# U turned onto the feature partitions by TensorE, and the first loads regrouped, in a two-layer conditioned residual kernel

## The chip, the cores and the metric

One NeuronCore of a Trainium2 chip. The metric is the device time of one execution in microseconds. The kernel before took 618.98 us (median of 3 runs, 617.96 to 619.11).

## The reference

B = 2, S = 2048, D = 512, RANK = 30. Two layers, each added to its input:

```python
# layer 0: a linear map of low rank that depends on the batch
U = (cond_512 @ W_dec + b_dec).reshape(B, 513, 30)     # cond_512 [2, 256], W_dec [256, 15390]
param = einsum('bik,kj->bij', U, V)                    # V [30, 512]
x = x + einsum('bsd,bde->bse', x, param[:, :-1]) + param[:, -1][:, None]
# layer 1: six views of x, concatenated, through an MLP with layer norms
h = ln(ln(x, pw_g[path], pw_b[path]), cp_g[comp], cp_b[comp])
t = ln(x, tm_g[comp], tm_b[comp]);  s = ln(x, ms_g[scale], ms_b[scale])
m, n, r = (x + mlp_ln(state)[:, None] for state in (cond_512, cond_64, fside))
w = softmax(aw)
x = x + mlp_ln(concat([w[0]*h, w[1]*t, w[2]*m, w[3]*n, w[4]*r, w[5]*s]))   # W1 [3072, 512], W2 [512, 512]
```

## The kernel before

The 4096 rows are 32 tiles of 128 rows, alternating between the batches. Five engines each run an instruction list written out by hand and meet only at semaphores; the order in each list is the order of the work. Products that need accuracy are three float32r products (high x high, high x low, low x high) of 128x512; small set-up products are plain f32.

Start-up on TensorE, in its order (L759 to L955):
- 16 decode steps (`decode`, L724). Each multiplies cond, 32 columns per chunk, with a 960 KB block of W_dec (four concurrent products of 480 columns). Two steps make one eighth of U as rows: partition c*32+b holds batch b of feature chunk c. ScalarE copies each eighth to `Ur` (`evacuate`, L546).
- Behind nine of the steps a `prefill` (L749): twelve products of the x part of layer 1 for tiles 2 to 13. The x weights are the sum of the m, n and r blocks of W1, scaled by the softmax (`wx_first` L521 on ScalarE, `wx_add` L1166 and `wx_low` L1174 on VectorE), from the 12 tiles `mnr`.
- Then prefill 9, the first MLP product (L774, L775), prefill 10, the transposes of its result (L877), `embed` of tile 0 (L794), which needs the stacked U (`Ust`), prefill 11, `expand` of tile 0 (L804), the second MLP products (L866) and the phases of tiles 0 to 2. `sum_parts` (L873), `low_rank_product` (L885) and `offset_product` (L897) stand between them.

U has to stand with features on the partitions. `to_features` (L376) does that with 16 transfers, each from one row of `Ur` to 64 partitions with 30 numbers each: eight when half of U has been copied, eight when all has. GpSimd issues 12 of them before its other work, ScalarE 4. VectorE then adds the bias (L1234) and writes the stack (L1237, L1239) that `embed` needs.

For tile 0, VectorE sums x1 (L1276) and takes its statistics (L1249, L1253); GpSimd makes 1/sqrt from the variance (L1021 to L1034), but only after the low halves of x of tiles 0 and 1 (`x_low`, L1070); ScalarE makes xhat (L640); VectorE scales it to tt and st; TensorE transposes these (L737).

Loads: SP's queue carries the 12 mnr tiles, then W_dec blocks mixed with x^T tiles (`stash`), the MLP weights, the T, S and H blocks of W1 and W2 as ring slots come free, and for each tile x, its indices and index rows (`idxrep`, two broadcasts to 64 partitions). ScalarE's queue carries aw, all constants (`cst`, 1203 columns: cond, identity, bias, V^T, then the picking matrices and others), V, wlast and the MLP biases.

Of the kernel before, what the change touches and what calls it, by code (L numbers as in the profile page):

```python
# [25 lines left out]
ALU = mybir.AluOpType  # L26
# [5 lines left out]
RANK = 30  # L32
# [95 lines left out]
def build(nc, d, out):  # L128
# [11 lines left out]
    with ExitStack() as ctx:  # L140
# [46 lines left out]
        aw = sb("aw", [P, 6])  # L187
# [62 lines left out]
        mnr = sb_at(at_mnr, "mnr", [P, 3, KC, D])  # L250


        V4, wlast = stash[:, NPRE - 1, :], stash[:, NPRE - 2, 0:2 * P].rearrange("p (c r) -> p c r", r=P)
# [18 lines left out]
        XU, XV = bank[0:2]  # L272
        TP, HID, OUT = bank[2:4], bank[4:6], bank[6:8]
# [6 lines left out]
        aw_in, cst_in, late_in, mlp_in = sem("aw_in"), sem("cst_in"), sem("late_in"), sem("mlp_rows_in")  # L280
# [8 lines left out]
        u_in_pool, u_in_act = sem("u_in_pool"), sem("u_in_act")  # L289
# [86 lines left out]
        def to_features(eng, got, half, rows):  # L376

            eng.wait_ge(u_row, DECS // 2 * (half + 1))
            at, n = half * P // 2, P // 2
            load(eng, got, *[(Uf[at:at + n, b, c, :],  # L380
                              Ur[c * Q + b:c * Q + b + 1, at * RANK:(at + n) * RANK].rearrange(
                                  "o (p r) -> o p r", r=RANK)) for c, b in rows])

        U_ROWS = [(c, b) for c in range(KC) for b in range(B)]

# [4 lines left out]
        def _(sp):  # L390
# [26 lines left out]
            def load_rows(a):  # L417
# [15 lines left out]
                for half in range(2):  # L433
                    sp.dma_start(idxrep[half * P // 2:(half + 1) * P // 2, s, :],
                                 d["rows"][s, half, bass.ds(pair, 1), :].to_broadcast([P // 2, P])) \
                      .then_inc(rep_in[s], 16)

            for c in range(KC):
                for k, src in enumerate((WM, WN, WR)):
                    load(sp, mnr_in[c], (mnr[:, k, c, :], d["int_W1"][src * D + c * P:src * D + (c + 1) * P, :]))  # L440
            for j in range(2 * DECS):
# [18 lines left out]
            load_x(Tile(1))  # L460
            sp.wait_ge(dec_used, 2 * DECS)
# [48 lines left out]
        def _(act):  # L510
            load(act, aw_in, (aw[:, :], d["aw"].to_broadcast([P, 6])))
            load(act, cst_in, (cst[:, :], d["cst"]))
            load(act, late_in, (V4, d["V4"]), (wlast, d["wlast"].rearrange("(c p) r -> p c r", p=P)))
# [7 lines left out]
            def wx_first(c):  # L521
                act.wait_ge(mnr_in[c], 48)
                nc.scalar.activation(wx[:, c, :], mnr[:, 0, c, :], ACT.Copy, scale=wsm[:, WM:WM + 1]).then_inc(wx_m, 1)
# [52 lines left out]
            to_features(act, u_in_act, 1, U_ROWS[KC:])  # L576
# [146 lines left out]
        def _(pe):  # L723
# [34 lines left out]

            pe.wait_ge(cst_in, 16)  # L759
            for j in range(2 * DECS):  # L760
                decode(j)
                if j == 0:

                    pe.wait_ge(late_in, 32)
# [105 lines left out]
            def sum_parts(sel, got, done, start=True):  # L870

                pe.wait_ge(got, 1)
# [7 lines left out]
            def low_rank_product():  # L880

                pe.wait_ge(lm_ready, 2)
                for k in range(3):
                    for c in range(KC):
                        nc.tensor.matmul(pPART[c * Q:(c + 1) * Q, :], LM[:, k, c, :], mnr[:, k, c, :],  # L885
# [5 lines left out]
            def offset_product():  # L891

                pe.wait_ge(vw_part, 1)
# [113 lines left out]
        def _(pool):  # L1007
# [85 lines left out]
            to_features(pool, u_in_pool, 0, U_ROWS)  # L1093
# [508 lines left out]
```

## Time and profile before

| | |
|---|---|
| profiled execution | 619.02 us, its span 617.2 us |
| TensorE busy | 586.1 us, 95% |
| GpSimd, VectorE, ScalarE busy | 390.1, 417.5, 204.2 us |
| mean granted clock of TensorE | 0.997 |
| HBM over the span | 164 GB/s |
| first product of TensorE | 18.06 us |

PE is TensorE, PEld its weight loads, DVE VectorE, ACT ScalarE, POOL GpSimd, SP the engine that issues most transfers; SPq, ACTq and POOLq are the issues of a transfer. L731 is line 731 of the kernel before. A group of instructions names the tile written and the tiles read. A plain f32 product appears as two weight loads and two multiplies. Times count from the start of the span. `ring` holds W_dec and later weights, `bank` is PSUM.

### The profile page before, as it was taken

The numbers are of one execution on the slowest core, as the hardware profiler recorded it, in microseconds if no ns is written. First come the engines' busy times: TensorE is split into PE (matmuls) and PEld (weight loads), VectorE is DVE, ScalarE is ACT, GpSimd is POOL, SyncE is SP. The second block draws the span as 40 slices with busy tenths as digits, with TensorE's granted clock in tenths as the row PEclk, the third lists the DMA queues.
The fourth block names the chain that finished last, engine by engine and source line by source line (L and its number), as shares of the span: only waits on it lengthen the run. The fifth ranks groups of instructions, "written<-read, shape, count | busy, mean of one in ns | idle before, by whom it ended". The sixth has DMA issues, their size and how long they took to land.

```text
span 617.2 us, 9159 instructions
## 1 busy us (share of the span) xinstructions
PE 586.1 (95%) x2924; PEld 454.5 (74%) x2924; DVE 417.5 (68%) x750; ACT 204.2 (33%) x346; POOL 390.1 (63%) x499
## 2 busy tenths in 40 slices
PE   0899979999999999999999999999999999999995
PEld 0455436488888888888888888788888888888784
DVE  3411277588888888888766766776666666667754
ACT  3333344334333334333232233233223332332222
POOL 1002447668888888888776667666776766666720
PEclk9999999999999999999999999999999999999998
DMA  8999898434454455555424344445443433344201
GB/s 292 404 403 381 302 356 282 126 90 140 142 172 145 142 148 159 172 157 176 146 90 122 121 139 140 109 139 140 140 130 99 135 125 123 124 140 112 81 19 51
DMA packets 53119, 102.07 MB, mean 165 GB/s; under 512 B 10446, under 2 KB 23246, under 8 KB 52956
## 3 DMA queue, kind: packets, MB, share of 16 engines
q1 hardware_dynamic: 39872, 58.52, 28.0%
q0 software_dynamic: 12160, 42.04, 22.3%
q10 hardware_dynamic: 1052, 1.07, 0.5%
q8 instruction: 18, 0.29, 0.2%
q14 instruction: 17, 0.14, 0.1%
HBM read 93.10 MB, written 8.39 MB: 164 GB/s over the span
## 4 chain that ended last, share of the span: by engine, by line
PE 68%; POOL 7%; issue 7%; DMA 7%; DVE 6%; SPq 2%; ACT 2%; POOLq 0%; DVEq 0%; ACTq 0%
PE bank L743 18%; PE bank L744 18%; PE bank L745 18%; PE bank L737 7%; DMA xraw<-in_xT 2%; PE bank L731 2%; DMA ring<-in_W_dec 2%; DMA ring<-in_int_W 2%; PE bank L794 2%; SPq L332 2%; DVE bn L1249 2%; POOL rs L1029 1%; POOL h L1081 1%; POOL h L1079 1%; POOL ctt L1046 1%
## 5 line engine op out<-in xcount | busy, mean ns | idle before, releaser
L743 PE MATMUL bank<-W,ops 128*128 128x512 f32 x432 | 178.4, 413 | 0.1
L744 PE MATMUL bank<-W,ops 128*128 128x512 f32 x432 | 171.4, 397 | 0.0
L745 PE MATMUL bank<-W,ops 128*128 128x512 f32 x432 | 171.1, 396 | 0.0
L591 ACT ACTIVATE ops<-bank 128x512 fp32r<-128x512 f32 x97 | 57.0, 589 | 154.1 <-PE bank L737 152.4
L743 PEld LDWEIGHTS bank<-W,ops 128*128 128x128 f32 x432 | 81.8, 189 | 25.4 <-issue 7.3
L745 PEld LDWEIGHTS bank<-W,ops 128*128 128x128 f32 x432 | 81.7, 189 | 20.0
L744 PEld LDWEIGHTS bank<-W,ops 128*128 128x128 f32 x432 | 81.9, 190 | 14.8
L1244 DVE TENSOR_TENSOR ops<-bank,ops 128x512 fp32r<-128x512 f32 x97 | 66.1, 683 | 11.7 <-ACT ops L591 11.7
L1249 DVE BATCH_NORM_STATS2 bn<-h 128x6 f32<-128x512 f32 x32 | 22.2, 692 | 55.2 <-POOL h L1081 55.2
L1021 POOL TENSOR_SCALAR ve<-mv 128x1 f32<-128x1 f32 x94 | 31.4, 334 | 38.5 <-DVE mv L1253 34.8
L640 ACT ACTIVATE xhat<-x,nm,rs 128x512 f32<-128x512 f32 x32 | 26.1, 815 | 81.0 <-POOL nm L1034 81.0
L743 PE MATMUL bank<-W,zop 128*128 128x512 f32 x124 | 49.6, 400 | 0.4 <-DVE zop L1244 0.4
L1081 POOL TENSOR_TENSOR h<-h,pwt 128x512 f32<-128x512 f32 x32 | 47.6, 1488 | 2.5
L744 PE MATMUL bank<-W,zop 128*128 128x512 f32 x124 | 49.0, 395 | 0.0
L745 PE MATMUL bank<-W,zop 128*128 128x512 f32 x124 | 49.0, 395 | 0.0
L1070 POOL TENSOR_TENSOR xop<-stash,xop 128x512 fp32r<-128x512 f32 x18 | 23.2, 1289 | 39.5 <-ACT xop L562 39.5
L1370 DVE SCALAR_TENSOR_TENSOR o<-o,mv,gbc 128x512 f32<-128x512 f32 x31 | 47.6, 1537 | 0.0
L1046 POOL DMA_INDIRECT ctt<-in_ct,idx x32 | 40.6, 1270 | 9.4 <-issue 5.9
L1079 POOL TENSOR_TENSOR h<-xhat,pwt 128x512 f32<-128x512 f32 x32 | 42.7, 1335 | 2.9 <-ACT xhat L640 1.9
L647 ACT ACTIVATE ht<-h,nm,rs 128x512 f32<-128x512 f32 x32 | 26.1, 816 | 55.2 <-POOL nm L1034 55.2
L332 POOL DMA_DIRECT2D Uf<-Ur x12 | 6.5, 563 | 58.6 <-ACT Ur L548 58.6
L1046 POOL DMA_INDIRECT sgt<-in_ms_g,idx x32 | 35.4, 1105 | 11.4 <-issue 11.4
(145 smaller groups left out, 1089.3 us busy)
## 6 DMA issues: line engine op xcount, KB each, us to landing
ring<-in_W_dec SPq DMA_DIRECT2D x16, 960.0 KB, 12.5
x<-in_x SPq DMA_DIRECT2D x32, 256.0 KB
out<-xb SPq DMA_DIRECT2D x31, 256.0 KB
stash<-in_xT SPq DMA_DIRECT2D x30, 256.0 KB, 6.3
ring<-in_int_W SPq DMA_DIRECT2D x4, 1024.0 KB, 11.7
xraw<-in_xT SPq DMA_DIRECT2D x14, 256.0 KB
mnr<-in_int_W SPq DMA_DIRECT2D x12, 256.0 KB, 8.0
idxrep<-in_rows SPq DMA_DIRECT2D x64, 32.0 KB
```

The costliest lines, as they stand in the source:

```text
L591: nc.scalar.activation(dst.rearrange("p c t -> p (c t)"), bank[:, :], ACT.Copy).then_inc(done, 1)
L737: last = nc.tensor.transpose(dst[:, c * P:(c + 1) * P], src[:, c * P:(c + 1) * P], ident)
L743: nc.tensor.matmul(bank[:, :], op[:, HI, c, :], w[:, HI, c, :], start=start and c == 0, stop=False)
L744: nc.tensor.matmul(bank[:, :], op[:, HI, c, :], w[:, LO, c, :], start=False, stop=False)
L745: last = nc.tensor.matmul(bank[:, :], op[:, LO, c, :], w[:, HI, c, :], start=False, stop=stop and c == KC - 1)
L1021: nc.gpsimd.tensor_scalar(ve[:, which:which + 1], mv[:, which, 1:2], EPS, 1.0, ALU.add, ALU.mult) \
L1046: pool.indirect_dma_start(out=dst[:, s, :], out_offset=None, in_=d[table], in_offset=bass.IndirectOffsetOnAxis(ap=idx[:, s, col:col + 1], ...
L1079: nc.gpsimd.tensor_tensor(h1[:, :], xhat[:, :], pwt[:, s, 0:D], ALU.mult).then_inc(h1_part, 1)
L1081: nc.gpsimd.tensor_tensor(h1[:, :], h1[:, :], pwt[:, s, D:2 * D], ALU.add).then_inc(h1_ready, 1)
L1244: nc.vector.tensor_tensor(dst.rearrange("p c t -> p (c t)"), bank[:, :], hi.bitcast(F32).rearrange("p c t -> p (c t)"), ALU.subtract).then ...
L1249: nc.vector.bn_stats(bn[:, which, :], src).then_inc(bn_done, 1)
L1370: nc.vector.scalar_tensor_tensor(out=o[:, :], in0=o[:, :], scalar=mv[:, 2, 0:1], in1=gbc[:, :], op0=ALU.subtract, op1=ALU.mult).then_inc(u ...
```

## The change

The sixteen transfers go. After the last decode step TensorE waits until all of U has been copied and multiplies: for each of the 30 ranks r, the weights are the 128 columns `Ur[:, p*30 + r]` (a step of 30 numbers), the moving operand eight columns of the identity, which pick the rows c*32+b. The results stand in one PSUM bank; VectorE reads them there when it adds the bias. The low halves of stash tiles 10 and 11 (`pre_low`), made ahead of the stack of U until now, are made behind it.

mnr is stored in the order of loading: 4 loads of 768 KB with 6 KB rows, not 12 of 256 KB. aw stands ahead of the first (64 bytes per row, 16 numbers), already repeated on 128 rows. The constants are loaded in two parts by SP: columns 0 to 507 ahead of the last mnr load, the rest (`picks_in`) after tile 1's x; four places wait for it. V and wlast become one load behind the first W_dec block. The index rows are stored repeated, one load of 128 rows per tile. Stash tiles 10 and 11 are loaded ahead of tile 0's rows.

```diff
+        URT = bank[0][:, 0:RANK * B * KC]
-        def to_features(eng, got, half, rows):
-            eng.wait_ge(u_row, DECS // 2 * (half + 1))
...
+            def turn_u():
+                pe.wait_ge(u_row, DECS)
+                for r in range(RANK):
+                    last = nc.tensor.matmul(URT[:, r * B * KC:(r + 1) * B * KC],
+                                            Ur.rearrange("q (p r) -> q r p", r=RANK)[:, r, :],
+                                            ident.rearrange("p (c q) -> p q c", q=Q)[:, 0:B, :], start=True, stop=True)
+                last.then_inc(u_turned, 1)
...
                 if j in PRE_AFTER:
                     prefill(PRE_AFTER.index(j))
+            turn_u()
             prefill(NPRE - 3)
...
# SP
-            for c in range(KC):
-                for k, src in enumerate((WM, WN, WR)):
-                    load(sp, mnr_in[c], (mnr[:, k, c, :], d["int_W1"][...]))
+            load(sp, mnr_in[0], (mnr_row[:, 0:P // 8 + 3 * D], d["mnr"][:, 0:P // 8 + 3 * D]))
+            for c in range(1, KC):
+                if c == KC - 1:
+                    load(sp, cst_in, (cst[:, 0:AT_BL], d["cst"][:, 0:AT_BL]))
+                load(sp, mnr_in[c], (mnr[:, c, :, :], d["mnr"][...]))
...
                 load_ring(sp, DEC[j])
+                if j == 0:
+                    load(sp, late_in, (late, d["late"]))
...
-            load_rows(Tile(0))
             load_pre(NPRE - 2)
             load_pre(NPRE - 1)
+            load_rows(Tile(0))
...
             load_x(Tile(1))
+            load(sp, picks_in, (cst[:, AT_BL:CST], d["cst"][:, AT_BL:CST]))
# ScalarE
-            load(act, aw_in, (aw[:, :], d["aw"].to_broadcast([P, 6])))
-            load(act, cst_in, (cst[:, :], d["cst"]))
-            load(act, late_in, (V4, d["V4"]), (wlast, d["wlast"]...))
-            to_features(act, u_in_act, 1, U_ROWS[KC:])
# GpSimd
-            to_features(pool, u_in_pool, 0, U_ROWS)
-            to_features(pool, u_in_pool, 1, U_ROWS[:KC])
# VectorE
-            v.wait_ge(aw_in, 16)
+            v.wait_ge(mnr_in[0], 16)
-            for p in range(2, NPRE - 1):
+            for p in range(2, NPRE - 2):
                 pre_low(p)
-            pre_low(NPRE - 1)
-            v.wait_ge(u_in_pool, 16 * 3 * KC)
-            v.wait_ge(u_in_act, 16 * KC)
+            v.wait_ge(u_turned, 1)
             for b in range(B):
-                last = nc.vector.tensor_tensor(Uf[:, b, :, :], Uf[:, b, :, :], bdec[:, :, :], ALU.add)
+                last = nc.vector.tensor_tensor(
+                    Uf[:, b, :, :], URT.rearrange("p (r b c) -> p b c r", b=B, c=KC)[:, b, :, :], bdec[:, :, :], ALU.add)
...
+            pre_low(NPRE - 2)
+            pre_low(NPRE - 1)
```

## Rows read from the trace of the kernel before

**Rows 1.** The page's first part: busy us, share of the span, instructions.

```profile
PE 586.1 (95%) x2924; PEld 454.5 (74%) x2924; DVE 417.5 (68%) x750; ACT 204.2 (33%) x346; POOL 390.1 (63%) x499
```

**Rows 2.** TensorE's waits, 0 to 140 us: us in total, times, longest.

```profile
PE bank L731 <- DMA ring<-in_W_dec: 18.7, 3, 18.1
PE bank L873 <- ACT part L595: 2.4, 2, 1.5
PE bank L794 <- POOL xop L1070: 1.5, 1, 1.5
PE bank L866 <- DMA ring<-in_mem_W: 0.8, 1, 0.8
PE bank L794 <- DVE Ust L1239: 0.6, 1, 0.6
```

**Rows 3.** Busy time by stretch; last: granted clock, DMA share, GB/s.

```profile
2.00:5.00 3.00, 0.00 (x0) 0.00 (x0) 0.00 (x0) 0.90 (x1) 0.51 (x3) 1.00 0.65 148
8.00:16.00 8.00, 0.00 (x0) 0.00 (x0) 5.11 (x8) 3.67 (x6) 0.00 (x0) 1.00 1.06 384
16.00:50.00 34.00, 31.72 (x157) 17.46 (x158) 10.51 (x19) 11.52 (x22) 3.49 (x7) 1.00 1.05 403
50.00:55.00 5.00, 5.00 (x26) 3.17 (x26) 0.69 (x1) 1.59 (x3) 0.92 (x2) 1.00 1.07 367
66.00:69.00 3.00, 3.00 (x11) 1.31 (x11) 0.00 (x0) 0.00 (x0) 2.18 (x5) 1.00 0.52 135
```

**Rows 4.** Timeline of TensorE's decode steps: start us, us, what, wait before.

```profile
21.06 1.83 PE L731 MATMUL bank<-ring,cst 128*32 128x480 f32 x8 [0.22 <-DMA ring<-in_W_dec]
63.62 1.01 PE L731 MATMUL bank<-ring,cst 128*32 128x480 f32 x8 [0.37 <-DMA ring<-in_W_dec]
```

**Rows 5.** Transfer issues, 0 to 140 us: count, KB each, median us to landing.

```profile
ring<-in_W_dec SPq DMA_DIRECT2D x16, 960.0 KB, 12.5
mnr<-in_int_W SPq DMA_DIRECT2D x12, 256.0 KB, 8.0
...
cst<-in_cst ACTq DMA_DIRECT2D x1, 601.5 KB, 6.5
...
stash<-in_V ACTq DMA_DIRECT2D x1, 256.0 KB, 7.4
```

**Rows 6.** Timeline of VectorE: the last two low halves of wx.

```profile
17.88 1.47 DVE L1176 TENSOR_TENSOR W<-wx,W 128x512 fp32r<-128x512 f32 x2
```

**Rows 7.** Timeline of ScalarE: the last copy of U's sums.

```profile
64.70 0.57 ACT L548 ACTIVATE Ur<-bank 128x480 f32<-128x480 f32 x1 [1.10 <-PE bank L731]
```

**Rows 8.** Timelines of TensorE and its weight loads (PEld): f32 loads, grouped.

```profile
19.82 1.01 PE L766 MATMUL bank<-cst,stash 128*128 128x2 f32 x4
...
75.13 0.32 PEld L877 LDWEIGHTS bank<-cst,part 6*128 6x128 f32 x4 [0.37 <-issue]
...
111.16 0.30 PEld L873 LDWEIGHTS bank<-part,cst 128*128 128x128 f32 x2
```

**Rows 9.** Groups of weight loads, 0 to 140 us: busy us, mean ns of one.

```profile
L873 PEld LDWEIGHTS bank<-part,cst 128*128 128x128 f32 x4 | 0.6, 188 | 1.1 <-issue 1.1
...
L877 PEld LDWEIGHTS bank<-cst,part 6*128 6x128 f32 x4 | 0.3, 136 | 0.4 <-issue 0.4
```

**Rows 10.** Timelines of VectorE and GpSimd: tile 0's sums, variance, tile 1's low half.

```profile
80.42 0.68 DVE L1276 TENSOR_TENSOR x<-bank,x 128x512 f32<-128x512 f32 x1
81.94 0.18 DVE L1253 BATCH_NORM_AGGREGATE mv<-bn 128x2 f32<-128x6 f32 x1
...
81.97 1.26 POOL L1070 TENSOR_TENSOR xop<-xraw,xop 128x512 fp32r<-128x512 f32 x1 [8.52 <-ACT xop L562]
```

**Rows 11.** Chain that ended last: start us, us, what.

```profile
24.04 0.43 PE bank L745
...
29.68 0.24 PE bank L744
```

**Rows 12.** Busy time by stretch at the kernel's end, columns as in rows 3.

```profile
613.00:614.00 1.00, 0.00 (x0) 0.00 (x0) 0.92 (x2) 0.29 (x1) 0.00 (x0) 0.87 0.53 199
```

More of the change, by code:

```diff
@@ L249, in build @@
         assert cursor[0] - at_mnr >= 3 * BLOCK
-        mnr = sb_at(at_mnr, "mnr", [P, 3, KC, D])
-        V4, wlast = stash[:, NPRE - 1, :], stash[:, NPRE - 2, 0:2 * P].rearrange("p (c r) -> p c r", r=P)
+        mnr_row = sb_at(at_mnr - 4 * P // 8, "mnr_row", [P, P // 8 + KC * 3 * D])
+        aw, mnr = mnr_row[:, P // 8 - 6:P // 8], mnr_row[:, P // 8:].rearrange("p (c k n) -> p c k n", k=3, n=D)
+        late = stash[:, NPRE - 2:NPRE, :].rearrange("p a n -> p (a n)")[:, D - 2 * P:2 * D]
+        V4, wlast = late[:, 2 * P:2 * P + D], late[:, 0:2 * P].rearrange("p (c r) -> p c r", r=P)
         def x_rows(a):
@@ L374, in u_bank_of @@
             return pU[m % len(pU)]
-        def to_features(eng, got, half, rows):
-            eng.wait_ge(u_row, DECS // 2 * (half + 1))
[L379 to L384, printed above, removed]
         block = ctx.enter_context(nc.Block())
@@ L432, in load_rows @@
                     sp.wait_ge(oh_ready, read)
[L433 to L436, printed above, removed]
-            for c in range(KC):
-                for k, src in enumerate((WM, WN, WR)):
-                    load(sp, mnr_in[c], (mnr[:, k, c, :], d["int_W1"][src * D + c * P:src * D + (c + 1) * P, :]))
+                sp.dma_start(idxrep[:, s, :], d["rows"][s, bass.ds(pair, 1), :, :].rearrange("o p n -> (o p) n")) \
+                  .then_inc(rep_in[s], 16)
+            load(sp, mnr_in[0], (mnr_row[:, 0:P // 8 + 3 * D], d["mnr"][:, 0:P // 8 + 3 * D]))
+            for c in range(1, KC):
+                if c == KC - 1:
+                    load(sp, cst_in, (cst[:, 0:AT_BL], d["cst"][:, 0:AT_BL]))
+                load(sp, mnr_in[c], (mnr[:, c, :, :], d["mnr"][:, P // 8 + c * 3 * D:P // 8 + (c + 1) * 3 * D].rearrange(
+                    "p (k n) -> p k n", n=D)))
             for j in range(2 * DECS):
@@ L521, in wx_first @@
             def wx_first(c):
-                act.wait_ge(mnr_in[c], 48)
-                nc.scalar.activation(wx[:, c, :], mnr[:, 0, c, :], ACT.Copy, scale=wsm[:, WM:WM + 1]).then_inc(wx_m, 1)
+                act.wait_ge(mnr_in[c], 16)
+                nc.scalar.activation(wx[:, c, :], mnr[:, c, 0, :], ACT.Copy, scale=wsm[:, WM:WM + 1]).then_inc(wx_m, 1)
             def wx_high(c):
@@ L1344, in split_bt @@
             def split_bt():
+                v.wait_ge(picks_in, 16)
                 v.wait_ge(bt_high, 1)
@@ L1577 @@
         "idx": np.stack([path, comp, scale], axis=-1),
-        "rows": np.stack([scale, comp], axis=1),
+        "rows": np.repeat(np.stack([scale, comp], axis=2), P // 2, axis=2),
         "cst": cst,
         "int_b1": L1["int_b1"][None], "int_b2": L1["int_b2"][None], "int_g": L1["int_g"][None],
-        "int_be": L1["int_be"][None], "aw": L1["aw"][None],
+        "int_be": L1["int_be"][None],
+        "mnr": np.concatenate([np.zeros((P, P // 8 - 6), np.float32), np.broadcast_to(L1["aw"][None], (P, 6)), np.stack(
+            [chunks(L1["int_W1"][src * D:(src + 1) * D]) for src in (WM, WN, WR)], axis=2).reshape(P, -1)], axis=1),
         "mlp_W1": chunks(put(2 * MU, D, (0, 0, L1["mem_W1"]), (MU, 0, L1["noi_W1"]), (MU + P, 0, L1["res_W1"]))),
@@ L1584 @@
         "mlp_b2": np.repeat(np.stack([L1[f"{m}_b2"] for m in mlps]), B, axis=0),
-        "wlast": put(MU, P, *[(0, q * Q, W_dec[:, NDEC:]) for q in (0, 2, 3)]),
         "W_dec": W_dec,
-        "V4": put(P, D, *[(q * Q, 0, V) for q in range(4)]),
+        "late": np.concatenate([flat(chunks(put(MU, P, *[(0, q * Q, W_dec[:, NDEC:]) for q in (0, 2, 3)]))),
+                                put(P, D, *[(q * Q, 0, V) for q in range(4)])], axis=1),
         "pw": np.concatenate([L1["pw_g"], L1["pw_b"]], axis=1),
```

23 lines of the change are left out of this document (12 added, 11 removed).

## The prediction

> **What bounds the kernel now.** I read the page's busy shares first, then TensorE's waits in the first 140 us, then the chain, the transfer rates by stretch, and the timelines of each engine from 61 to 110 us.
>
> TensorE is busy for 95% of the span [rows 1]. Its waits over 0.5 us are few and all lie early: 18.7 us for W_dec (18.1 of them before its first product), 2.4 for the copied partial sums, 1.5 for the low half of tile 1's x, 0.8 for the second MLP's weights and 0.6 for the stacked U [rows 2]. From 125 us on it hardly waits, so the steady part moves as a block: what TensorE loses or wins before 110 us is the whole change in time. I therefore look for how much later or earlier it reaches tile 1's transposes (about 110 us), where the start-up ends.
>
> The start is bound by transfers. They move 148 GB/s from 2 to 5 us, 384 from 8 to 16 and 403 later [rows 3]; TensorE's second decode step waits until 21.06 us for its block of W_dec and the first prefill follows at once [rows 4]. From there to 61 us it never waits for over 0.1 us. The transfers keep pace, and only the last block is late: 0.37 us at 63.62 [rows 4].
>
> **Part 1, the order of the first loads.** Ahead of the second W_dec block the queues carry 12 x 256 KB of mnr, 601.5 of constants, 256 of V, about 31 small, and 960 + 960 of W_dec [rows 5], with 128 of wlast (256 x 128 numbers) and 256 of x (128 x 512): 6264 KB. After the change the constants are cut at column 508 of 1203, 254 KB, and the rest (347 KB) goes behind tile 1's x; aw adds 8 KB of padding and rides in the first wide load; V and wlast are one load of 384 behind the first block. That is 5922 KB. 342 KB less at 403 GB/s [rows 3] brings the second decode step 0.87 us forward. The first decode step gains more (726 KB, 1.8 us), but the prefill stands behind the second. The softmax of aw now waits for the 776 KB of the first wide load, at latest about 6 us; the chain of wx on ScalarE and VectorE then runs on, and has to end before the 20.2 at which the block lands. It was over at 19.35 before [rows 6], with nearly 1 MB more mixed into its loads, so even without the gain it is hidden.
>
> **Part 2, wide first loads.** Twelve issues become four, and the 128-row broadcast of aw and the constants leave ScalarE's queue. The queue was fed faster than it drained, so issue time is not the gain; the slow three microseconds at 148 GB/s are. If small rows cause all of it, it costs 3 x (1 - 148/403) = 1.9 us; if it is the way that a queue starts, nothing. Bounds 0 to 1.9, and 0.4 more if wide rows raise the 384 of 8 to 16 us to 403. I take 0.7, nearer to nothing, because 256 KB transfers with 2 KB rows run at 384 once the start is over [rows 3].
> The Trainium skill (DMA: Bandwidth & Descriptors, Rules for kernel authors) asks for 1 MiB or more per transfer, and its table has 78% of the peak at that size. Here transfers of 256 KB queued behind one another reach 384, so the measurement decides; by the page the wide loads would give the upper end.
>
> **Part 3, the old transfers of U go.** Sixteen small issues, twelve on GpSimd's queue and four on ScalarE's, vanish: eight when the first half of U is there, eight when the second is. The rate falls to 367 GB/s in 50 to 55 us, against 403 before [rows 3]: 0.45 us of stream. With it goes, I think, the 0.37 us wait for the last block. From 66 to 69 us the rate is 135 GB/s with much queued [rows 3]; that hole (2.0 us at 403) closes too, but it shortens the weights' way, not TensorE's, whose only wait there is 0.8 us. Neither engine's issue slots are on the path.
>
> **Part 4, the 30 products.** They stand on TensorE between the last decode step and prefill 9. First comes a stall: the last block's sums must be copied by ScalarE, which starts at 64.70 and takes 0.57 us [rows 7], while the decode step ended at about 64.56. With signalling 0.8 us. Behind the waiting products stand prefill 9, the first MLP product and everything later; nothing else can fill the gap.
> Each product with f32 data is two load-and-multiply pairs (L873: one product, two pairs). Eight columns are nothing, so the load sets the pace. One pair of full 128x128 f32 loads takes 0.30 us with 0.188 for one, which spaces them by 0.11 [rows 8, 9]. 60 x 0.11 = 6.6 us. Bounds: the 128-column loads of L877 come every (0.32 - 0.136)/3 = 0.061, in single passes: 3.7 us; L766, the nearest in kind (128x128 weights, 2 columns), takes 1.01 us for four, 0.25 each, at the low clock: 15.2 us, 7.6 if the high clock halves it. I take 6.6, by the nearest row at the high clock. So TensorE gets 7.4 us more.
>
> What VectorE gains or gets: the bias additions now read PSUM (two of 0.28 us), pre_low of tiles 10 and 11 moves behind them, 0.7 us each, and both are done within 3 us of the last product, before prefill 9 and the first MLP product, which stood together for 7.6 us, are over; it costs nothing. SP loads the last two stash tiles before tile 0's rows; gathers of tile 0 are needed 15 us later.
>
> **What absorbs it.** Entering prefill 9, TensorE is late by 7.4 - 0.87 - 0.37 - 0.7 = 5.5 us. Then:
> 1. The wait for the stacked U, 0.63 us, is gone [rows 2].
> 2. Tile 0's x1 on VectorE began at 80.42 [rows 10], 0.5 us after its product, because a weight split was running; it will be idle then.
> 3. GpSimd took tile 0's variance at 83.3 only because tile 1's low half, fed by a transfer, ended at 83.23, while the variance was there at 82.1 [rows 10]. 1.2 us of slack.
> So tile 0's tt, which TensorE transposed the moment it was ready, comes 5.5 - 2.3 = 3.2 us late. TensorE's own waits of 0.8, 1.5 and 1.5 [rows 2] are gaps within this chain and are not subtracted twice. From there the loads of the H block and of W2 follow TensorE and VectorE, with less queued ahead of them, and come at most as late as the rest. Small gaps before the last product of tile 0 and before tile 1's transposes, none over 0.5 us in the waits [rows 2], I count as 0.6 us in all.
> The index rows in one transfer instead of two save SP about 0.6 us of issuing per tile; SP is on no path in the steady part: nothing.
>
> **Sum.** 7.4 (products and stall) - 1.24 (parts 1 and 3) - 0.7 (part 2) - 2.3 - 0.6 = +2.6 us. The profiled execution took 619.02 us around a span of 617.2, and the median of the three timed runs is 618.98, so both give 621.6.
>
> **Rivals.**
> *A: the products are slower than 0.11 us a pair.* Two ways. The clock: from 18 to 26.4 us a 512-column product came every 0.43 us, later every 0.24 [rows 11], the 1.2 and 2.4 GHz levels. At the end of the kernel, with TensorE empty, the granted clock falls (0.87 in the mean of 613 to 614 us) [rows 12]. The turning lasts 7 us with products of eight columns; if those count as no work, the second half of the loads takes twice as long (+3.3) and prefill 9 runs at 0.43 (12 x 0.19 = +2.3). Against it: the array never stands empty, and neither the 0.8 us stall nor the longer waits at 80 to 92 us lowered the clock before. The other way is the operand: weights with a step of 30 elements, which no row here has. At twice the price, +6.6. Together 625 to 628. Chance 0.22.
> The Trainium skill says on the clock (TensorE: Matmul & The Clock Gate, Part 1) that the throttled rate is the default and activity lifts it. On the operand (SBUF — State Buffer, Door 1: The DMA port swizzle) it says that steps beyond 16 bytes lose bandwidth; a step here is 120 bytes. No row of this case shows either, and by the second the time is the 628.
> *B: no change that can be told.* Part 2 gives its full 1.9 + 0.4 instead of 0.7, and the sum is +1.0: 620.0. For it: at 148 GB/s the transfer engines were busy for 0.65 of the time [rows 3], so a third of the loss at least is not their limit. Chance 0.14.
> *C: faster.* The loads run at the 0.061 us of L877. The place is TensorE between 64 and 72 us; the extra work is then 4.5 us instead of 7.4 and the sum -0.3 with my start, -1.9 with the full one: 617.1 to 618.7. It decides once the turning takes less than about 4 us, or 5.3 with the full start. For it: multiplies of eight columns leave the array to the loads alone. Against it: the two-pair row of L873. Chance 0.18.
>
> **How the numbers follow.** My sum has 0.46: between 620.3 and 623.5. A measurement of this kernel tells 0.2%, 1.2 us, from no change. Of C's 0.18 two thirds lie beyond that, since loads that quick go best with a start that gives much (0.12 faster, 0.06 within); B adds 0.14 to no change; the sum and A are slower. So faster 0.12, within 0.2% 0.20, slower 0.68. The range goes to C's middle and well into A: 617.6 to 626.5.
>
> **What would show it.** 60 loads of the turning in one block of 6 to 7 us after a gap of 0.8; their spacing decides between the sum, A and C. The second decode step at 19.5 (20.2 without part 2). Prefill 9 at about 70 instead of 64.6; tile 0's first transposes 3 us later, at about 89.5; granted clock 1.00 throughout, else A. The 135 GB/s hole at 66 to 69 gone. The prediction fails if TensorE's delay is absorbed beyond 3.5 us before 110, which would mean that transfers bound that stretch.

## The result, and the profile after

The changed kernel took 629.42 us (median of 6 runs, 627.95 to 630.07), the kernel before 619.03 on the same chip (6 runs): ratio 1.0167, 95% interval [1.0152, 1.0181]. It is 10.4 us slower; forecast were 2.6, with a range that ended at 626.5. The profiled execution took 629.41 us around a span of 627.6.

The page's first part, for the kernel after (against [rows 1]):

```profile
PE 601.5 (96%) x2984; PEld 468.9 (75%) x2984; DVE 414.6 (66%) x750; ACT 204.5 (33%) x346; POOL 383.7 (61%) x487
```

TensorE has 60 multiplies more (30 products, two each) and is busy 15.4 us longer: the loss is work in its own line, not a new wait. Its waits in the first 140 us (line, source, us in total, times, longest; against [rows 2]):

```profile
PE bank L723 <- DMA ring<-in_W_dec: 16.2, 3, 14.5
PE bank L876 <- ACT part L587: 1.2, 2, 0.8
PE bank L796 <- POOL xop L1074: 0.8, 1, 0.8
PE bank L755 <- ACT Ur L541: 0.7, 1, 0.7
PE bank L729 <- DVE tt L1291: 0.2, 1, 0.2
```

All waits together fell from 24.0 [rows 2] to 19.1 us. The only new one of size is the 0.7 ahead of the turning (L755). Now TensorE's timeline (start us, us, line, what, wait before), where the decode steps answer to [rows 4]:

```profile
14.48 1.83 PE L723 MATMUL bank<-ring,cst 128*32 128x480 f32 x8 [14.48 <-DMA ring<-in_W_dec]
18.46 1.83 PE L723 MATMUL bank<-ring,cst 128*32 128x480 f32 x8 [1.20 <-DMA ring<-in_W_dec]
23.97 1.01 PE L723 MATMUL bank<-ring,cst 128*32 128x480 f32 x8
...
60.23 1.01 PE L723 MATMUL bank<-ring,cst 128*32 128x480 f32 x8 [0.51 <-DMA ring<-in_W_dec]
61.93 14.75 PE L755 MATMUL bank<-cst,Ur 128*128 128x8 f32 x60 [0.69 <-ACT Ur L541]
...
76.53 0.78 PE L735 MATMUL bank<-W,ops 128*128 128x512 f32 x1
...
81.05 3.60 PE L776 MATMUL bank<-ring,cst 128*6 128x512 f32 x8
...
97.93 0.66 PE L729 MATMUL bank<-cst,tt 128*128 128x128 f32 x4 [0.20 <-DVE tt L1291]
...
120.53 0.66 PE L729 MATMUL bank<-cst,tt 128*128 128x128 f32 x4
```

Two of the same places before (third decode step, first MLP product):

```profile
27.54 1.01 PE L731 MATMUL bank<-ring,cst 128*32 128x480 f32 x8
67.55 3.60 PE L774 MATMUL bank<-ring,cst 128*6 128x512 f32 x8
```

The second decode step comes 2.60 us earlier than before, the last 3.39. Then stands one block of 14.6 us with 60 multiplies of eight columns. Prefill 9 starts at 76.53 (before 64.56, 11.97 late), the first MLP product at 81.05 (67.55, 13.50 late), tile 0's transposes come at 97.93 (86.48, 11.45 late) and tile 1's at 120.53 (109.87, 10.66 late). The span is 10.4 longer, so from there on nearly everything moves as one piece, as the prediction took it (a small gain behind it is the subject of e13).

The group of weight loads that sets the block's pace, 55 to 90 us (busy us, mean ns of one, then the idle time before):

```profile
L755 PEld LDWEIGHTS bank<-cst,Ur 128*128 128x128 f32 x60 | 14.7, 341 | 1.5 <-ACT Ur L541 1.5
```

Each load takes 341 ns where the same shape took 188 [rows 9], and the loads come every (14.65 - 0.34) / 59 = 0.243 us. The stretches, columns as in [rows 3] (granted clock, DMA share, GB/s last):

```profile
2.00:5.00 3.00, 0.00 (x0) 0.00 (x0) 0.00 (x0) 1.27 (x1) 0.52 (x3) 1.00 0.91 336
8.00:16.00 8.00, 1.52 (x8) 0.23 (x8) 7.44 (x11) 3.85 (x6) 0.00 (x0) 1.00 1.02 394
50.00:55.00 5.00, 5.00 (x28) 3.10 (x25) 1.39 (x2) 2.08 (x5) 0.00 (x0) 1.00 1.05 405
62.00:63.00 1.00, 1.00 (x5) 1.00 (x5) 0.00 (x0) 0.00 (x0) 0.00 (x0) 0.94 0.91 338
63.00:64.00 1.00, 1.00 (x6) 1.00 (x5) 0.00 (x0) 0.05 (x1) 0.00 (x0) 0.50 1.05 389
70.00:71.00 1.00, 1.00 (x6) 1.00 (x6) 0.00 (x0) 0.00 (x0) 0.89 (x2) 0.50 1.06 398
79.00:80.00 1.00, 1.00 (x4) 0.80 (x3) 0.00 (x0) 0.00 (x0) 0.00 (x0) 0.53 1.04 383
66.00:69.00 3.00, 3.00 (x14) 3.00 (x14) 0.00 (x0) 0.00 (x0) 1.83 (x2) 0.50 1.02 380
```

Three things stand in it. The transfers start at 336 GB/s instead of 148. The hole at 66 to 69 us (135) is gone. And one microsecond into the turning the granted clock falls to 0.50 (1.2 GHz) and comes back only at 79.9, behind two thirds of prefill 9. The block has five or six multiplies per microsecond (those cut by an edge counted in both) at 0.94 and at 0.50 alike. The stretch at the high clock is short, one microsecond, so whether the clock or the operand makes the pace is what the experiments had to tell apart. What answers to [rows 7] and [rows 10], the last copy of U on ScalarE and tile 0 on VectorE and GpSimd:

```profile
61.31 0.57 ACT L541 ACTIVATE Ur<-bank 128x480 f32<-128x480 f32 x1 [1.24 <-PE bank L723]
```

```profile
91.94 1.29 DVE L1219 SCALAR_TENSOR_TENSOR W<-ring,wsm,W 128x1024 fp32r<-128x1024 f32 x1 [0.68 <-ACT W L575]
93.14 0.68 DVE L1279 TENSOR_TENSOR x<-bank,x 128x512 f32<-128x512 f32 x1
...
94.66 0.18 DVE L1256 BATCH_NORM_AGGREGATE mv<-bn 128x2 f32<-128x6 f32 x1
```

```profile
92.50 1.86 POOL L1074 TENSOR_TENSOR xop<-xraw,xop 128x512 fp32r<-128x512 f32 x1 [20.57 <-ACT xop L555]
95.02 0.19 POOL L1025 TENSOR_SCALAR ve<-mv 128x1 f32<-128x1 f32 x1 [0.66 <-DVE mv L1256]
```

GpSimd now waits for VectorE (0.66 us) and no longer the other way round. x1 still starts the moment that a split of weights (L1219) ends.

### The profile page after: what moved, and what is told of

Same layout as the page of the kernel before. It is cut to its first block, busy times and chain, and to the rows that moved or that the text cites. A ratio compares the mean times of both kernels' runs of the same rounds, so it can differ in the third digit from the quotient of the medians.

```text
span 627.6 us, 9196 instructions
## 1 busy us (share of the span) xinstructions
PE 601.5 (96%) x2984; PEld 468.9 (75%) x2984; DVE 414.6 (66%) x750; ACT 204.5 (33%) x346; POOL 383.7 (61%) x487
## 4 chain that ended last, share of the span: by engine, by line
PE 70%; POOL 9%; DMA 8%; DVE 5%; issue 4%; ACT 2%; SPq 1%; DVEq 0%; POOLq 0%
PE bank L735 18%; PE bank L737 18%; PE bank L736 18%; PE bank L729 6%; DMA ring<-in_W_dec 4%; DMA pwt<-in_pw,idx 4%; PE bank L755 2%; POOL h L1085 2%; PE bank L796 2%; PE bank L723 2%; DVE bn L1252 2%; POOL h L1083 2%; POOL rs L1033 1%; POOL ctt L1050 1%; POOL ve L1025 1%
## 5 line engine op out<-in xcount | busy, mean ns | idle before, releaser
L1247 DVE TENSOR_TENSOR ops<-bank,ops 128x512 fp32r<-128x512 f32 x97 | 66.2, 683 | 10.8 <-ACT ops L583 10.6
L1375 DVE SCALAR_TENSOR_TENSOR o<-o,mv,gbc 128x512 f32<-128x512 f32 x31 | 46.2, 1489 | 0.0
L1094 POOL TENSOR_TENSOR xb<-x,bebc 128x512 f32<-128x512 f32 x32 | 42.0, 1314 | 0.6
```

Source lines behind the costliest of these rows:

```text
L1094: nc.gpsimd.tensor_tensor(xb[:, f.row, :], x1[:, f.slot, :], bebc[:, :], ALU.add).then_inc(xb_ready, 1)
L1247: nc.vector.tensor_tensor(dst.rearrange("p c t -> p (c t)"), bank[:, :], hi.bitcast(F32).rearrange("p c t -> p (c t)"), ALU.subtract).then ...
L1375: nc.vector.scalar_tensor_tensor(out=o[:, :], in0=o[:, :], scalar=mv[:, 2, 0:1], in1=gbc[:, :], op0=ALU.subtract, op1=ALU.mult).then_inc(u ...
```

## The experiments

My theory after the result: the weights' step of 30 numbers makes a load slow, at either clock (rival A's second way). The rival: the low clock does it, and the operand nothing. The start has several possible causes too (width of the loads, their order, the index rows); these come after the products.

**The two halves of the change.** e1 is the changed kernel with its new loads and index rows, but with the 16 transfers of U back in place of the products:

```diff
-            turn_u()
...
+            to_features(pool, u_in_pool, 0, U_ROWS)
+            to_features(pool, u_in_pool, 1, U_ROWS[:KC])
...
+            to_features(act, u_in_act, 1, U_ROWS[KC:])
```

> The changed loads without the products: U goes back through the 16 transfers, everything else is the changed kernel. Theory (the products cost, the start gains): the changed kernel reached the end of its last decode step 3.4 us earlier (61.2 against 64.6), and TensorE then meets tile 0's chain again, so of the 3.4 about 2 to 3.4 stay: 615.6 to 617 us. Rival (the loads themselves cost something later, such as the constants behind tile 1's x): no faster than before, 619 or more.

e2 is the kernel before with the products in place of the transfers, its loads untouched but for stash tiles 10 and 11, which come ahead of tile 0's rows (and VectorE's low halves of these two tiles, made behind U as in the change):

```diff
+            turn_u()
...
-            to_features(pool, u_in_pool, 0, U_ROWS)
...
```

> The 30 products in the kernel before, with its old loads (its stash tiles 10 and 11 loaded ahead of tile 0's rows, as in the change). Theory (the products' 14.7 us, a stall of 0.8 and a prefill at the low clock, +1.5, less 3 us absorbed before 110 us): +13 to +14, so 632 to 633. Rival (the products cost less with the old loads because the transfers bound that stretch): under 629.

e1 took 614.15 us against 618.53 (ratio 0.9925 [0.9909, 0.9942]), e2 633.99 (1.0240 [1.0223, 1.0257]). In the profiled spans that is -4.8 and +15.6, together +10.8 where the whole change has +10.4: the halves add up. e1 came out faster than its theory (614.15, expected were 615.6 to 617), e2 slower (633.99, expected 632 to 633). The block in e2 is the block of the changed kernel, so the crowd of transfers around it, which differs, does nothing to it. But the clock falls later in it, at 68.2 us, three microseconds in, so it has a longer stretch at the high clock (the two microseconds with columns as above):

```profile
65.27 14.74 PE L753 MATMUL bank<-cst,Ur 128*128 128x8 f32 x60 [0.69 <-ACT Ur L539]
...
67.00:68.00 1.00, 1.00 (x6) 1.00 (x6) 0.00 (x0) 0.07 (x1) 0.00 (x0) 1.00 1.04 393
72.00:73.00 1.00, 1.00 (x5) 1.00 (x5) 0.00 (x0) 0.00 (x0) 0.85 (x1) 0.50 1.04 403
```

The same products with the same operands keep five to six multiplies per microsecond at 1.00 and at 0.50. So the clock does not make the pace of the block.

**Clock against operand.** e3 moves 128 identity columns instead of eight, the weights keep their step:

```diff
-                    last = nc.tensor.matmul(URT[:, r * B * KC:(r + 1) * B * KC],
+                    last = nc.tensor.matmul(bank[0][:, r * B * KC:r * B * KC + P],
                                             Ur.rearrange("q (p r) -> q r p", r=RANK)[:, r, :],
-                                            ident.rearrange("p (c q) -> p q c", q=Q)[:, 0:B, :], start=True, stop=True)
+                                            ident.rearrange("p (c q) -> p q c", q=Q), start=True, stop=True)
```

> The changed kernel with 128 columns of the identity as moving operand in each of the 30 products, not 8, the 8 wanted ones first; each product overwrites what the one before wrote beyond them, so U comes out the same. The weights keep their step of 30 numbers. Theory stride (the strided load takes 0.34 us and comes every 0.24 whatever the clock): the block still takes about 14.6 us; the clock stays high, so only prefill 9 gains its 1.5 us: 627.5 to 628. Rival clock (the low clock doubled the loads): the block falls to about 7.3 us and the time to 620 to 621.

It took 628.04 us (1.0154 [1.0137, 1.0171]), 1.4 less than the changed kernel; the two were measured on different chips and their intervals overlap, but in the traces tile 1's transposes also come 1.4 us earlier (119.11 against 120.53). The block lasted 15.04 us, and these are two of its microseconds (columns as above):

```profile
65.00:66.00 1.00, 1.00 (x6) 1.00 (x5) 0.00 (x0) 0.00 (x0) 0.00 (x0) 0.50 0.99 246
70.00:71.00 1.00, 1.00 (x6) 1.00 (x6) 0.00 (x0) 0.00 (x0) 0.88 (x2) 1.00 1.04 406
```

The clock fell at 64 us and was back at 67.5, inside the block. The pace was five to six loads per microsecond at 1.00, at 0.50 and at 1.00 again. By itself e3 says little of the eight-column products, because its 128 moving columns are stepped too and e4 will show that these alone hold a pair at 0.22 us; the proof for them is e2. What e3 adds is the price of the clock: the slow prefill 9 behind the block, which e3 does not pay (4.52 us for prefill 9 after the change, 2.99 before: 1.5).

e4 and e5 make the weights contiguous: ScalarE writes U rank by rank, e4 with 128 moving columns and e5 with the eight of the change.

```diff
-                nc.scalar.activation(Ur[:, m * BANK:(m + 1) * BANK], u_bank_of(m)[:, 0:BANK], ACT.Copy) \
+                nc.scalar.activation(Ur.rearrange("q (r p) -> q p r", r=RANK)[:, m * BANK // RANK:(m + 1) * BANK // RANK, :],
+                                     u_bank_of(m)[:, 0:BANK].rearrange("q (p r) -> q p r", r=RANK), ACT.Copy) \
...
-                                            Ur.rearrange("q (p r) -> q r p", r=RANK)[:, r, :],
+                                            Ur[:, r * P:(r + 1) * P],
```

> As the wide one (128 moving columns), and ScalarE writes U so that the 128 weights of one rank lie side by side. Theory stride: the loads come every 0.11 us, the block takes 6.5 us at the high clock, prefill 9 runs at 0.24 per product: 8 + 1.5 us less than the changed kernel, 619.5 to 620.5. Rival clock alone: the same as the wide strided one. Were both needed, the strided wide one would lie between.

> The changed kernel with the 128 weights of each rank side by side (ScalarE's copy writes U rank by rank) and the eight strided columns of the identity as in the change. The strided kernel with 128 columns and the high clock kept 0.24 us per pair, so the loads' step is one limit; side by side and with 128 strided moving columns it was still 0.22, with the load itself down from 0.34 to 0.23. Theory (two strided operands, each alone enough to halve the pace): eight columns can't hold the loads up, so the pairs come every 0.11 us while the clock is high and 0.2 to 0.25 after it has fallen, as L766 before; the clock falls as in the change, so the block takes 11 to 13 us and the time is 626 to 628. Rival (the pace of 0.22 is the price of any weight load with plain f32 products in a row): the block takes 13.2 us or more and the time stays within 1 us of 628.

e4 took 626.62 us (1.0124 [1.0107, 1.0141]), e5 626.19 (1.0118 [1.0096, 1.0141]). e4's block is still 13.59 us, so its theory (6.5 us, 619.5 to 620.5) failed; e5's is 10.96. The wait ahead of the block grew from 0.69 to 1.09, because ScalarE's last copy, now written with a step, takes 0.97 us instead of 0.57. Three microseconds of e5:

```profile
63.00:64.00 1.00, 1.00 (x11) 1.00 (x11) 0.00 (x0) 0.00 (x0) 0.00 (x0) 1.00 0.97 354
65.00:66.00 1.00, 1.00 (x7) 1.00 (x6) 0.00 (x0) 0.17 (x1) 0.00 (x0) 0.50 1.08 231
70.00:71.00 1.00, 1.00 (x6) 1.00 (x7) 0.00 (x0) 0.00 (x0) 0.89 (x2) 0.50 1.05 406
```

Here a pair comes every 0.11 us, the price that the prediction had put on it, until the clock falls; then every 0.21. The one edit between e5 and the changed kernel is how the weights lie, and at the high clock it takes a pair from 0.24 us to 0.11: the step of the weights is the cause. With contiguous weights the clock decides the rest; stepped ones keep 0.24 at either clock. e4 shows a second price. Its weights are contiguous too, but its 128 moving columns are read with a step of 32 numbers, and the block takes 13.59 / 60 = 0.227 us a pair, most of it at the high clock.

e6 reads both operands contiguously (its edit against e4). Its eight columns are then not the eight that are wanted, so it leaves out the picking of the rows; it serves for the time of the block alone:

```diff
-                                            ident.rearrange("p (c q) -> p q c", q=Q), start=True, stop=True)
+                                            ident, start=True, stop=True)
```

> Weights side by side and the identity's 128 columns in their own order as moving operand, so both operands are read without a step and the clock should stay high. What it leaves wrong is U: its eight columns are not the eight wanted ones. Theory (two strided operands): pairs every 0.11 us, the block 6.5 to 7.5 us, 619.5 to 621. Rival (any f32 weight load costs 0.22): block 13, time 626 to 627.

619.49 us (1.0015 [1.0004, 1.0025]). The groups of weight loads of e4 (first) and e6 (busy us, mean ns) show that the step of the moving columns comes back in the loads, which take 232 ns with it and 192 without:

```profile
L756 PEld LDWEIGHTS bank<-cst,Ur 128*128 128x128 f32 x60 | 12.5, 232 | 2.7 <-ACT Ur L541 1.9
```

```profile
L756 PEld LDWEIGHTS bank<-cst,Ur 128*128 128x128 f32 x60 | 6.8, 192 | 1.9 <-ACT Ur L541 1.9
```

In e6 the block is 6.96 us, 0.115 a pair, and the clock stayed at 1.00. This is the block that was forecast (6.6), and the loads take the 0.19 us of [rows 9].

**The turning made as cheap as I could.** e7 uses transpose mode (one load-and-multiply pair per product instead of two) with contiguous weights and stepped columns; e9 the same with the picking order stored as a permutation matrix, so that neither operand has a step; e10 puts e9's block behind the first MLP product; e11 is e1 again, beside e9 and e10 on the same chip. The edit of e9 against e4:

```diff
+        perm = cst[:, AT_PERM:AT_INQUAD]
...
-                                            ident.rearrange("p (c q) -> p q c", q=Q), start=True, stop=True)
+                                            perm, is_transpose=True)
```

> Weights side by side and the 30 products in transpose mode, in which an f32 product is one pair and not two; the moving operand is all 128 columns of the identity, the eight wanted ones first, so still with a step. Theory: 30 pairs at 0.11 (a strided f32 moving operand costs about twice the 0.053 of 128 columns) to 0.22 us, 3.3 to 6.6 us in all; with the clock kept high 616 to 620. Rival (transpose mode doesn't count as activity and the clock falls): 1.5 us more, and the granted clock shows it.

> Differs from the changed kernel in the turning alone: ScalarE writes U number by number (contiguous weights), the 30 products run in transpose mode, one pass each, and the moving operand is a stored permutation of 128 columns without a step. The theory (a step costs on each operand, whatever the clock): 30 pairs at about 0.1 us, so a block of 3 to 3.5 us instead of 14.75 and some 3.5 us less than the 6.86 us of the same kernel with a stepped moving operand; with the start's 4.4 us gained, about 616 us against 619 before. The rival (a product costs 0.22 us in transpose mode whatever its operands): block again 6.9 us, 619.7 us.

> As the kernel with the stored permutation, but the turning is issued after the first product of the MLP rows and ahead of prefill 10, so ScalarE's last copy of U has more than 5 us to be done. If the wait ahead of the block (0.7 to 1.1 us) is paid in full, about 615 us; if VectorE's and GpSimd's work on U then ends later than TensorE needs it (first embedding), no gain or 1 us of loss, 616 to 617 us.

> The kernel with the new first loads and the old 16 transfers of U, without the products, again, for a comparison on one chip: 614.2 us by its first runs. If turning U on TensorE with plain operands costs less there than the transfers' waits, the two kernels beside it are faster than this one; expected is the reverse, by 1 to 2 us, because the transfers ran beside TensorE's work and the products stand in its line.

| | us | ratio to before | block |
|---|---|---|---|
| e7 stepped columns | 619.69 | 1.0014 [1.0004, 1.0025] | 6.86 us, 30 products |
| e9 no step | 616.11 | 0.9954 [0.9939, 0.9968] | 3.50 us |
| e10 no step, later | 615.08 | 0.9941 [0.9926, 0.9955] | 3.49 us |
| e11 transfers of U | 614.00 | 0.9920 [0.9906, 0.9935] | none |

```profile
62.92 3.50 PE L758 MATMUL bank<-cst,Ur 128*128 128x128 f32 x30 [1.09 <-ACT Ur L543]
```

```profile
68.72 3.49 PE L758 MATMUL bank<-cst,Ur 128*128 128x128 f32 x30
```

The first line is e9, the second e10, whose block has no wait ahead. The step of the columns costs 3.4 us over 30 products, and placing the block behind other work saves the 1.1 us of waiting. Even so the turning on TensorE ends 1.1 us behind the transfers that it replaces (615.08 against 614.00; the ranges of the six executions of each do not overlap). The transfers ran beside TensorE's work, and the one wait that they leave is that for the stacked U, here in e11:

```profile
PE bank L797 <- DVE Ust L1245: 1.6, 1, 1.6
```

The 1.1 us isn't the products alone: the stored permutation makes the first part of the constants 64 KB larger, and e9's and e10's second decode steps come at 19.01 and 18.90 us, e11's at 18.49. How much of that reaches the end was not measured.

The fastest kernel found is the new start with the old transfers; in e11 it took 614.00 us against 618.75 of the kernel before, 4.8 us less (4.0 to 5.8 by the interval).

**What in the start gains.** e8 is e1 with mnr again as twelve loads of 256 KB with 2 KB rows, in the new order, and aw in a small load of its own ahead of them:

```diff
-            load(sp, mnr_in[0], (mnr_row[:, 0:P // 8 + 3 * D], d["mnr"][:, 0:P // 8 + 3 * D]))
+            load(sp, mnr_in[0], (mnr_row[:, 0:P // 8], d["mnr"][:, 0:P // 8]))
+            def narrow(c):
+                load(sp, mnr_in[c], *[(mnr[:, c, k, :], d["int_W1"][src * D + c * P:src * D + (c + 1) * P, :])
+                                      for k, src in enumerate((WM, WN, WR))])
+            narrow(0)
...
+                narrow(c)
```

> The kernel with the changed loads and the old 16 transfers of U (614.15 us), but the mnr blocks again as 12 loads of 256 KB with 2 KB rows, in the new order and with aw as a load of 64 bytes per row ahead of them. Theory order (what counts is 342 KB less ahead of the second W_dec block and no small-row loads on ScalarE's queue): 614 to 614.8, with 300 GB/s or more from 2 to 5 us. Theory width (6 KB rows fill the queues sooner): the second decode step back at about 20 us and 615.5 to 616, with 150 to 200 GB/s from 2 to 5.

615.54 us (0.9943 [0.9925, 0.9961]), 1.4 us slower than e1 and 1.5 than e11, the same kernel on e8's chip; the intervals of the ratios just overlap. Its second decode step comes at 20.43, e1's at 18.57, the kernel before's at 21.06: the order gives 0.63 us there, the width 1.86. At the end of the last decode step e8 is 1.40 us ahead of the kernel before (63.23 against 64.63), e1 2.69 (61.94), so of the width 1.3 are left there. From 2 to 5 us the narrow loads moved 271 GB/s, e1's wide ones 317, the old start 148 [rows 3]: most of the old hole in the rate closes with the new order and queue, before any load gets wider.

e12 is the kernel before with nothing but the new index rows:

```diff
-                for half in range(2):
-                    sp.dma_start(idxrep[half * P // 2:(half + 1) * P // 2, s, :],
-                                 d["rows"][s, half, bass.ds(pair, 1), :].to_broadcast([P // 2, P])) \
-                      .then_inc(rep_in[s], 16)
+                sp.dma_start(idxrep[:, s, :], d["rows"][s, bass.ds(pair, 1), :, :].rearrange("o p n -> (o p) n")) \
+                  .then_inc(rep_in[s], 16)
```

> The kernel before with nothing changed but the index rows: stored repeated, one load of 128 rows per tile instead of two broadcasts to 64 partitions. In the steady part the traces of the kernel before and of the one with the products alone repeat every 16.91 us, those of all kernels with the new index rows every 16.83; within a tile the 0.08 us comes in the twelve products with the x operand. The theory (the two broadcasts slow that stretch, though SP is on no path): 16.83 us per tile here too, and, with about 18 such tiles, 1.3 to 1.6 us less, 617.3 us against 618.7. The rival (the index rows do nothing, as predicted; the period comes from the start's new order of buffers): 16.91 and 618.7 us.

617.46 us (0.9970 [0.9958, 0.9982]), 1.9 us faster, but not where I expected it. The period of a tile stayed at 16.91 us; the gain is in the start. The hole, two of TensorE's waits in the first 140 us, and tile 1's transposes in e12, which stood at 109.87 before:

```profile
66.00:69.00 3.00, 3.00 (x11) 1.14 (x10) 0.02 (x1) 0.68 (x2) 2.33 (x5) 1.00 0.95 328
```

```profile
PE bank L792 <- DVE Ust L1237: 1.4, 1, 1.4
...
PE bank L792 <- POOL xop L1068: 0.8, 1, 0.8
```

```profile
108.08 0.66 PE L735 MATMUL bank<-cst,tt 128*128 128x128 f32 x4
416.47 0.60 PE L735 MATMUL bank<-cst,tt 128*128 128x128 f32 x4
433.38 0.60 PE L735 MATMUL bank<-cst,tt 128*128 128x128 f32 x4
```

The rate from 66 to 69 us is 328 GB/s with all 16 transfers of U still there. So the two broadcasts of index rows made the hole (135) of [rows 3]. e2 says the same from the other side: it has no transfers of U but still the broadcasts, and its hole is only shifted, from 68 to 71 us, here its middle:

```profile
69.00:70.00 1.00, 1.00 (x6) 1.00 (x5) 0.00 (x0) 0.00 (x0) 0.00 (x0) 0.50 0.19 62
```

With the hole gone TensorE waits 0.8 us for the low half of tile 1's x, not 1.5 [rows 2], 1.2 for the copied partial sums, not 2.4, and no longer for the second MLP's weights; its wait for the stacked U grew from 0.6 to 1.4. That the hole made these waits by way of late transfers is argued, not shown step by step.

The period itself was still open. From the fifteenth tile on, sixteen periods in a row are 16.91 us (two of them 17.0) in the kernels with the old start and 16.83 (two of them 16.9) in those with the new one; the eleven periods ahead of these take 14.1 us in both, single ones up to 14.9. The new start takes `aw` (24 bytes) out of the row of tiles, which puts all tiles behind it 32 bytes lower in SBUF. e13 is the kernel before with that alone, no instruction changed:

```diff
-        aw = sb("aw", [P, 6])
...
         VWst = sb("VWst", [P, D], F32R)
+        aw = sb("aw", [P, 6])
```

> The kernel before with one tile moved: aw (6 numbers) is placed behind all others, so that every tile placed after it in SBUF starts 32 bytes lower, as in the changed kernel. No instruction differs. The theory (the period of 16.91 us in the steady part against 16.83 in the kernels with the new start comes from where the tiles stand): 16.83 us per tile, and 618.0 instead of 618.9 us, about 1 us over the steady part. The rival (the places of the tiles do nothing): 16.91 and 618.9.

617.62 us (0.9974 [0.9963, 0.9984]). TensorE's transposes of tt in e13, and below in the kernel before:

```profile
418.10 0.60 PE L737 MATMUL bank<-cst,tt 128*128 128x128 f32 x4
434.94 0.60 PE L737 MATMUL bank<-cst,tt 128*128 128x128 f32 x4
```

```profile
109.87 0.65 PE L737 MATMUL bank<-cst,tt 128*128 128x128 f32 x4
...
418.01 0.60 PE L737 MATMUL bank<-cst,tt 128*128 128x128 f32 x4
434.92 0.60 PE L737 MATMUL bank<-cst,tt 128*128 128x128 f32 x4
```

16.84 against 16.91: the places of the tiles make the period. Sixteen periods give 1.3 us; in the medians it is 1.5 (interval 1.0 to 2.3), in the profiled spans 0.8, because one tile of e13's profiled execution, among these earlier ones, took 14.94, the longest of them.

## Why the prediction was wrong

By its own terms, in us of TensorE's time:

| term | forecast | measured |
|---|---|---|
| lead at the last decode step (parts 1, 2, 3) | 1.94 | 3.39 |
| extra wait ahead of the products | 0.8 | 0.76 |
| 60 pairs | 6.6 | 14.6 |
| prefill 9 at the low clock | 0 | 1.5 |
| absorbed until tile 1's transposes | 2.9 | 2.84 |
| sum at tile 1's transposes | +2.6 | +10.7 |

(The lead and what is absorbed count against the rest.)

- **The step that failed is part 4's price of a pair, 0.11 us.** It came from L873 [rows 8, 9], whose weights are contiguous; the products of the change read theirs with a step of 30 numbers and take 0.243. The block alone is 8.0 us dearer than forecast, and the whole miss was 7.8: the other errors cancel. e2 shows that it is the products and not the clock, e5 that contiguous weights bring 0.11 at the high clock. The price stood inside the part's bounds (15.2 us by L766), and rival A's second way names this very mechanism, at twice the price where 2.2 times was measured; with 0.22 rival A was given too little. The row that I took had the right clock and size and the wrong operand, and I called it the nearest.
- On the operand the Trainium skill (SBUF — State Buffer, Door 1: The DMA port swizzle) says that steps beyond 16 bytes lose bandwidth. The runs agree, for weights (0.243 against 0.11 us) and for 128 moving columns (0.227 against 0.115, e4 and e6).
- **The clock** (rival A's first way) fell as that rival feared, though the array never stood empty. It cost 1.5 us on prefill 9, of the 2.3 that I had priced, and nothing within the block. The slow pace at the start (0.43 us a product from 18 to 26.4 us), which I had read as the 1.2 GHz level, lies in a stretch whose granted clock is 1.00 in the profile [rows 3], so that reading stands on the pace alone.
- **Part 1** came out at the second decode step: 0.63 us for the order, forecast 0.87. The aw chain was hidden, as said.
- **Part 2 was sized too small**: 0.7 taken, 1.86 us of TensorE's start measured by e8 against e1, the upper end. The Trainium skill (DMA: Bandwidth & Descriptors, Rules for kernel authors) asks for large transfers; here the run speaks for the page, against my reading of the 384 GB/s of [rows 3], which was taken after the start. Of the 1.86, 1.3 were left at the last decode step and 1.4 in the time. The wait for the stacked U took nothing of it: it is 1.5 us in e8 and 1.3 in e1 (0.6 before [rows 2]).
- **Part 3**: the rate at 50 to 55 us rose from 367 to 405 as said, but the last block is still waited for, 0.51 us. The lead grew from 2.60 us at the second decode step to 3.39 at the last, by more than the 0.37 that I gave this part; in both kernels the last step waits for its block, so this is the lead of the transfers. How much of it the transfers of U cost is not clear: the last decode step ends at 61.94 and 61.83 in e1 and e11, which have them, at 61.24 in the changed kernel, and between 61.12 and 61.83 in the seven others that have the new start without them. TensorE's own pace moves here as well: in the first prefill behind the second decode step nine of twelve products kept the slow pace of 0.43 us before the change and four after it, which alone takes the lead to 3.57 at the third decode step. Over all runs it is four to ten whatever the start, so this is luck of the profiled execution. The hole at 66 to 69 us closed for another reason than I gave: the index rows (e12, e2).
- **Index rows, put at nothing**, are worth 1.9 us to the kernel before. I looked for their price on SP and in the steady part, and it lay in the start-up, in the hole that I had seen and given to the wrong transfers. In the changed kernel they are worth nothing in that stretch, so for it the term was right. e2 has the old index rows and still takes as long from the first MLP product to tile 1's transposes as the changed kernel, 39.48 us (42.32 before, 40.88 in e12), with waits of 0.8 for xop and 1.1 for part:

```profile
85.26 3.60 PE L774 MATMUL bank<-ring,cst 128*6 128x512 f32 x8
...
124.74 0.66 PE L727 MATMUL bank<-cst,tt 128*128 128x128 f32 x4
```

- **What absorbs** was right in its total (2.84 us against 2.9) and half right in its parts. The 39.48 us stand, within 0.04, in e3 to e7 and e9 as well, whose blocks last between 3.5 and 15 us: once TensorE comes late enough, this stretch gives back 2.84 us and no more. The wait for the stacked U went, and so did GpSimd's lateness with tile 0's variance (1.2 forecast). VectorE was not idle before x1, as I had said it would be; the split that stood in its way moved along.
- **Not seen at all**: the 32 bytes, 1.3 us over sixteen tiles. e1's trace says where the new start gains its 4.4 us (4.8 in the spans): it is 2.68 us ahead at the first MLP product, 3.14 at tile 1's transposes and 4.8 at the end. So most is the lead of the first loads, about half of it by their width and half by order and queue (e8), at most 0.5 us lie where the index rows worked in e12, and 1.7 come behind, about what the 32 bytes give. The single edits (1.9 for the index rows, 1.5 for the places, 1.4 for the width) have nearly the same sum, but that is chance: of e12's gain at most 0.5 us is found in e1.
- Rival B lost with the block's price, though its start was the true one; C's 0.061 us never appeared.

## What to carry to other kernels

Price a new product by a row with the same access pattern, not only the same shape: weights or 128 moving columns read with a step of 30 or 32 numbers took TensorE's pace to half or less, and writing the tile in the order in which it will be read costs far less (here about 0.4 us more for each of ScalarE's eight copies, and 0.4 us more waiting of TensorE). Work put into the bounding engine's line must beat what it replaces in that line, not in total: 16 slow transfers beside TensorE cost it 1.6 us of waiting, and 30 products without a step 3.5 us of work. When a rate has a hole, find which transfers lie in it before giving its closing to an edit. And an edit's gain alone need not be its gain inside a larger change: compare the same stretch in both.

## What had not been expected of the hardware

- f32 weights with a step of 120 bytes load in 0.34 us and follow one another every 0.24, at a granted clock of 0.50 as at 1.00; contiguous ones every 0.11 at 1.00 and 0.21 at 0.50 (e5).
- 128 f32 columns moved with a step of 128 bytes took 0.22 us in transpose mode, contiguous ones 0.11 (e7, e9).
- The granted clock fell to 0.50 one to three microseconds into a block of back-to-back products in the changed kernel, e2, e3, e4, e5 and e7; in e3, e4 and e7 it was back at 1.00 by 68 us, inside the block, in the changed kernel (at 79.9), e2 and e5 only after it. In e6, e9 and e10 it never fell. Why it came back inside the one block and not the other is not settled.
- A ScalarE copy of 128x480 f32 from PSUM took 0.57 us, with the output stepped (512 bytes) 0.97 to 1.03.
- Tiles 32 bytes lower in SBUF shortened twelve products of each tile (those that read xop) by 0.08 us in all, with the same instructions (e13). Which tile it is, and why, was not tried.
- With two broadcasts of one row to 64 partitions (32 KB each) among the transfers, the queues moved 135 GB/s from 66 to 69 us; with one plain load of the same 64 KB, 328 (e12).
